# A mixer kernel on one core: unit 0's combination two scans later, the layer norm's shift one scan later, the normalising one slot later

## The reference

```python
x = x + 0.5 * ffn(layernorm(x), gate_w, experts)
x = x + mixer(layernorm(x), W_in, conv_w, conv_b, A_log, D, W_out)
x = x + 0.5 * ffn(layernorm(x), gate_w, experts)

def mixer(x, ...):
    x_ssm, res = split(x @ W_in.T)                  # 512 channels each
    x_conv = silu(causal_conv4(x_ssm) + conv_b)
    delta = softplus(x_conv)
    A_d = exp(delta[..., None] * -exp(A_log))       # 16 decays for each channel
    # for every channel and each of its 16 states, over the 2048 tokens:
    #   h = A_d[t] * h + x_conv[t]**2
    #   y[t] = x_conv[t] * sum(h over the 16 states)
    y = y * silu(res) + D * x_conv
    return y @ W_out.T
```

## Time and profile before

| | us |
|---|---|
| median of 3 runs | 3705.03 (3700.34 to 3710.84) |
| span of the profiled execution | 3705.3 |
| VectorE busy | 3111.1 (84%) |
| TensorE busy | 2776.9 (75%) |
| ScalarE busy | 2127.6 (57%) |
| GpSimd busy | 1324.0 (36%) |
| 512 scans on VectorE, line 1187 | 2224.4, 4.40 each |
| the chain that ends last | through the last layer |

### The profile page before, as it was taken

One profiled execution on the slowest core, in us unless ns is written; L12 is line 12 of the kernel. 1 busy time (PEld: TensorE's weight loads), 2 busy tenths in 40 slices (PEclk: granted clock), 3 DMA queues, 4 the chain that ended last, 5 costly groups with the idle time before them and its releaser, 6 DMA issues. The chain is left out here.

```text
span 3705.3 us, 29659 instructions
## 1 busy us (share of the span) xinstructions
PE 2776.9 (75%) x9252; PEld 1528.0 (41%) x9252; DVE 3111.1 (84%) x2547; ACT 2127.6 (57%) x2285; POOL 1324.0 (36%) x894
## 2 busy tenths in 40 slices
PE   8702688899889889889979979997896696035553
PEld 4502343354346346435534634543452455024442
DVE  6797579999999999999999999999999667982222
ACT  6300567876877777787687788778767362001111
POOL 0002265446245344534624434460111100035665
PEclk9655799999999899999989999999999896567776
DMA  7202277688678778868877787885686571034667
GB/s 276 106 0 81 78 174 178 144 182 185 150 165 161 178 163 177 191 135 173 179 162 170 158 180 160 177 193 118 127 153 132 113 282 83 0 117 132 218 221 244
DMA packets 146186, 575.75 MB, mean 155 GB/s; under 512 B 22096, under 2 KB 73872, under 8 KB 99216
## 3 DMA queue, kind: packets, MB, share of 16 engines
q0 software_dynamic: 76704, 400.61, 52.1%
q1 hardware_dynamic: 69360, 173.68, 12.7%
HBM read 154.72 MB, written 119.60 MB: 74 GB/s over the span
## 5 line engine op out<-in xcount | busy, mean ns | idle before, releaser
L1187 DVE TENSOR_TENSOR_SCAN state<-state,drive 128x2048 f32<-128x2048 f32 x512 | 2224.4, 4402 | 53.8 <-ACT state L1393 53.6
L1393 ACT ACTIVATE state<-delta,neg_a 128x2048 f32<-128x2048 f32 x512 | 1018.9, 2004 | 213.3 <-DMA delta<-xc 85.5
L1644 PE MATMUL ps_states<-state,ident 128*128 128x512 f32 x1792 | 843.2, 615 | 82.1 <-DMA state<-state 67.1
L1068 POOL DMA_DIRECT2D state<-state x255 | 235.6, 924 | 1299.9 <-DVE state L1187 1289.5
L1546 PE MATMUL ps_proj<-x1t,w_in 128*128 128x512 f32 x1024 | 507.3, 640 | 86.3 <-ACT xc L1342 30.4
L1644 PEld LDWEIGHTS ps_states<-state,ident 128*128 128x128 f32 x1792 | 344.5, 198 | 478.3 <-issue 381.6
L1562 PE MATMUL ps_proj<-conv_in,tap 128*128 128x512 f32 x1024 | 490.9, 631 | 53.6 <-ACT conv_in L1306 32.6
L997 POOL DMA_INDIRECT picked<-normed_rows,slot_now x112 | 356.7, 3185 | 95.0 <-PE ps_rows L1527 49.4
L1013 POOL DMA_INDIRECT x<-routed_rows,row_now x112 | 346.4, 3093 | 34.6 <-issue 34.6
L1546 PEld LDWEIGHTS ps_proj<-x1t,w_in 128*128 128x128 f32 x1024 | 204.2, 204 | 366.8 <-issue 273.2
L1562 PEld LDWEIGHTS ps_proj<-conv_in,tap 128*128 128x128 f32 x1024 | 205.0, 203 | 320.5 <-issue 281.9
(11 more groups left out here) (299 smaller groups left out, 3240.1 us busy)
## 6 DMA issues: line engine op xcount, KB each, us to landing
state<-state POOLq DMA_DIRECT2D x255, 1024.0 KB, 7.0
delta<-xc POOLq DMA_DIRECT2D x24, 1024.0 KB
normed_rows<-rows_in SPq DMA_DIRECT2D x8, 2048.0 KB
x_rows<-x SPq DMA_DIRECT2D x16, 1024.0 KB, 7.7
normed_rows<-rows_mid SPq DMA_DIRECT2D x8, 2048.0 KB
f_total<-x_rows SPq DMA_DIRECT2D x8, 2048.0 KB
routed_rows<-f_routed SPq DMA_DIRECT2D x128, 128.0 KB
out<-f_total SPq DMA_DIRECT2D x8, 2048.0 KB
```

Source lines behind the costliest of these rows:

```text
L1068: nc.gpsimd.dma_start(out=state[held(q)][:], in_=state[held(q - 1)][:], accum_op=ALU.add).then_inc(pair_landed(b, q // 2)[0], 16)
L1187: nc.vector.tensor_tensor_scan(state[held(q)][:], state[held(q)][:], drive[j % 2][:], 0.0, ALU.mult, ALU.add).then_inc(state_ready, 1)
L1393: nc.scalar.activation(state[held(q)][:], delta[j % 2][:], ACT.Exp, scale=g.neg_a[:, j, n:n + 1]).then_inc(decay_ready, 1)
L1644: mm = nc.tensor.matmul(ps_sum[c][:], g.ident[:], state[held(q)][:, c * CH:(c + 1) * CH], start=(opening and n == 1), stop=(n == N - 1))
```

## The change

Three numbers. Unit 0's combination stands behind scan 24 instead of 22. Both calls of `scales` (the shift) stand one scan later. Both normalisings start one slot later, with the slot of `deviation` as it was.

```diff
-    GATE, COMBINE = (3, 3, 4, 4), (6, 4, 6, 4)
+    GATE, COMBINE = (3, 3, 4, 4), (8, 4, 6, 4)
...
                         if q == SCALE[i]:
                             aggregate(b + 1, i)
-                        if q == SCALE[i] + 2:
+                        if q == SCALE[i] + 3:
                             scales(b + 1, i)
...
                             if q == SCALE[i] + 3:
                                 deviation(b + 1, i)
                             for t in range(TH):
-                                if q == SCALE[i] + 4 + t // 4:
+                                if q == SCALE[i] + 5 + t // 4:
                                     normalise(b + 1, i * TH + t)
```

## The result

| | before | after |
|---|---|---|
| median of 10 runs, us | 3703.99 (3689.77 to 3710.84) | 3715.7 (3703.76 to 3727.61) |
| span of the profiled execution | 3705.3 | 3713.7 |

The ratio of the changed kernel to the one before is 1.0037, with a 95% interval of 1.0023 to 1.0052: slower by 11.7 us on the medians and by some 14 us by the ratio, whose interval is about 9 to 19 us. The prediction was 3717.0 in a range of 3703 to 3729. Of the 19 runs of the kernel before that stand beside e5 to e8 one took 5033.5 us at a granted clock of 0.553, and the ratios leave it out.

The account below looks back on a forecast made before the run. The path was taken to go through GpSimd and DMA, not VectorE's own work. Batch terms (+4.2; +9.2 for 1, 5, 6; +3.2; -1.9 and -1.4; -1.3) gave +12.0 on 3705.3: 3717, range 3703 to 3729.

Parts of the forecast that it names:

- The path: Each batch runs through GpSimd's gathers, x, the DMA queue, `delta` and ScalarE's decays; `delta` lands 27.67 us behind x.
- Rival 3: The DMA queue absorbs x's delay and `delta` lands as now: about +0.3 us a batch, 3707 us; chance 0.07.
- The lock: A GpSimd gather that meets a running VectorE scan gets going only when the scan ends, ending about 0.84 us later.
- w: VectorE's wait for TensorE's last output projection before unit 0's combination; 0.88 to 2.97 us in batches 1 to 6.
- S: The moment scan 22 of a batch ends on VectorE, from which the times within that batch are counted.
- the free case: Gather of row 9 starts ahead of scan 26, takes 0.98 us, x issued at 17.4; border at w = 2.27.
- Rival 4: Scans don't hold up gathers, descriptor queue room does; x issued at 13.9, some 30 us faster, 3675 us; chance 0.10.
- Which gathers are free: Count of row 9 gathers ahead of scan 26: two, batches 2 and 4 (-1.9, -1.4 us); one or two: chance 0.36.
- locked: Gather of row 9 held until scan 26 ends; x 3.25 us later for w above 1.05, 3.4 for w = 0.88.
- rival 1: All gathers of row 9 locked, w below 2.27 throughout: +21.4 us in sum, 3727 us; chance 0.14.
- Batch 0: First batch, no wait before the combination: x issued at 20.4 instead of 16.06, 4.4 later, less 0.2: +4.2 us.
- Shift and normalising: VectorE's shift one scan and ScalarE's normalising one slot later: -0.2 us a batch, bounds -1.1 and +1.5.

Follow-up runs that it names:

- e5: Kernel before with GpSimd's transfer of x issued ahead of the gather of piece 8, nothing else moved: 3687.55 us, ratio 0.997.
- e8: Kernel before with only unit 0's combination moved, three scans later, behind scan 25: 3734.81 us against 3700.27, ratio 1.0087.
- e4: Changed kernel with GpSimd's transfer of x issued ahead of the gather of piece 8: 3679.72 us, ratio 0.9942 to the kernel before.
- e1: Kernel before with only unit 0's combination moved, behind scan 24: 3714.96 us against 3702.69, ratio 1.0036.
- e7: Changed kernel with 1.71 us of unused VectorE statistics added behind scan 25: 3698.86 us against the kernel before's 3700.27, ratio 1.0002.
- e9: Kernel before with the combination behind scan 24 and x issued ahead of the gather of piece 8: 3669.74 us, ratio 0.9907.
- e3: Kernel before with only unit 0's combination moved, one scan later, behind scan 23: 3683.94 us, ratio 0.9949.
- e2: Kernel before with only the shift one scan and the normalising one slot later: 3702.38 us, ratio 1.0001.
- e6: Kernel before with the combination behind scan 23 and x issued ahead of the gather of piece 8: 3659.6 us, ratio 0.989.
- e10: Kernel before with the combination behind scan 23, x ahead of the gather of piece 8, shift and normalising later: 3660.79 us, ratio 0.9889.

## Where the prediction held, and where not

**The path** (gathers of pieces 8 and 9, x, queue, `delta`, decays). Held. 13.9 of the 15.5 us by which the batches grew are landings; x to `delta` is 27.6 us as before in batches 1 to 6. Rival 3, that the queue absorbs the shift, would have had the landing at 46.1 in batch 5; it was at 47.9. e4 adds its limit: moving x alone earlier leaves the state transfer behind it where it was, and only part is handed on.

**The lock.** Held in its numbers. Gather 8 ends 5.20 us behind the combination's end (5.2 forecast), x follows 9.5 us behind it in batches 1 to 6. The prediction wrote that last as 10.8 for w = 2.31, or 20.4 behind S for small w, and w was small: 20.35. Gather 8 begins 1.0 us behind the combination's end and not 0.7; scan 25 hides the difference. In e1 the free case came out at 17.4 to the tenth, with the border case, w = 2.26, on the free side. Rival 4 needs gathers of about 1 us inside a running scan, with the descriptor queue's room as what held them. The interval from the state transfer's issue to the gather's end is 2140.29 - 2129.28 = 11.0 and 15.3 us after, where it was 4.58 and 8.84; no fixed room does this, and both gathers end 0.8 to 0.9 us behind scans as before. e7 closes it.

**Which gathers are free: this step failed.** The forecast carried each batch's w over from the trace of before and counted two free. After, w is 0.85 to 1.06 in all of batches 1 to 6, and all six are locked: rival 1's pattern. Rival 1 gave +22.7 for batches 0 to 6 though, and they grew by 15.5. Batch 0, which was not locked, makes 3.4 of the difference. The other cause is w: locked, x stands at 20.4 whatever w is below 1.05, so the price is 20.4 less where x stood before (w + 16.1), and not w + 19.4 less that. Over batches 1 to 6 the x transfers came 12.6 us later in sum and not 19.7; the growth that the landings don't explain, below, hides part of that. I had taken w out of the difference, as if it would be the same on both sides.

Part of where w comes from can be read in the row of TensorE's first eight convolutions after a pause of 4.4 us for ScalarE, some 110 us ahead of the combination that waits. Before, ahead of batch 6's w of 2.16 (2.27 by VectorE's wait):

```profile
2321.82 6.71 PE L1562 MATMUL ps_proj<-conv_in,tap 128*128 128x512 f32 x8 [4.44 <-ACT conv_in L1306]
```

and after, ahead of batch 6's w of 0.85:

```profile
2330.72 5.39 PE L1562 MATMUL ps_proj<-conv_in,tap 128*128 128x512 f32 x8 [4.45 <-ACT conv_in L1306]
```

The same eight matmuls, 1.32 us apart, and w is 1.31 apart. Stretches of 4 us over them, first of before and then of after: length; busy of PE, PEld, DVE, ACT, POOL; PEclk, DMA share, GB/s:

```profile
2322.00:2326.00 4.00, 4.00 (x5) 1.68 (x6) 4.00 (x3) 2.31 (x3) 1.81 (x2) 0.50 1.02 256
2326.00:2330.00 4.00, 4.00 (x8) 1.62 (x7) 4.00 (x2) 1.43 (x2) 2.50 (x1) 0.76 1.02 209
```

```profile
2331.00:2335.00 4.00, 4.00 (x6) 1.60 (x6) 4.00 (x3) 2.20 (x2) 1.92 (x2) 0.61 1.06 262
2335.00:2339.00 4.00, 4.00 (x14) 2.25 (x13) 4.00 (x2) 2.86 (x4) 2.39 (x1) 1.00 1.08 217
```

The granted clock is 0.50, the 1.2 GHz level, when TensorE takes up work after the pause. In the kernel before it stayed there for all of the first stretch; in the changed one it was back at 1.00, 2.4 GHz, sooner (0.61 is a mean over both levels). Over batches 1 to 6 of the twelve profiles a block of 5.1 to 5.4 us goes with w between 0.8 and 1.4, and one of 5.95 to 6.8 us with w of 1.65 to 3.0, but for four: 5.17 us with 2.95 (e1, batch 5), 5.19 with 2.93 (e8, batch 2), 5.48 with 2.48 (e7, batch 1) and 5.40 with 2.95 (e9, batch 5). So the time that the clock takes to come back after this pause goes with w in most batches, and it is not the only source of it. That the change made w small is not shown: e1, with the same combination, has three large ones.

**Batch 0.** Forecast +4.2, measured +0.8. This step failed too. The term came from "locked", since w is zero there. VectorE and GpSimd in batch 0 after:

```profile
578.88 8.74 DVE L1187 TENSOR_TENSOR_SCAN state<-state,drive 128x2048 f32<-128x2048 f32 x2 [2.41 <-ACT state L1393]
```

```profile
573.00 4.33 POOL L1013 DMA_INDIRECT x<-routed_rows,row_now  x1 [5.62 <-DVE xc L1168]
577.63 0.98 POOL L1013 DMA_INDIRECT x<-routed_rows,row_now  x1 [0.30 <-issue]
578.57 1.06 POOL L1022 DMA_DIRECT2D x<-in_x  x1
```

Scan 26 waits 2.41 us for its decay and starts at 17.6, so the gather, there at 16.4, is free. In the trace of before that decay ended at 15.1, which would have locked it. 1.5 of the 2.5 us between them lies again with TensorE behind a pause: eight matmuls that sum states, ahead of the projection that ScalarE waits for. Before and after:

```profile
565.10 3.67 PE L1644 MATMUL ps_states<-state,ident 128*128 128x512 f32 x8 [3.15 <-ACT ps_states L1335]
```

```profile
562.96 5.20 PE L1644 MATMUL ps_states<-state,ident 128*128 128x512 f32 x8 [3.15 <-ACT ps_states L1335]
```

The windows over their first 3.5 us, before and after:

```profile
565.10:568.61 3.51, 3.51 (x9) 1.60 (x10) 3.51 (x2) 3.40 (x4) 3.21 (x2) 1.00 0.73 149
```

```profile
562.96:566.50 3.54, 3.54 (x5) 1.67 (x6) 3.54 (x2) 3.41 (x4) 3.54 (x2) 0.56 0.54 111
```

The granted clock is 1.00 in the one and 0.56 in the other, behind the same pause of 3.15 us. e1, e3 and e8 have 5.18 us there, e2, e4, e5, e6, e7, e9 and e10 3.67. So both places where the forecast had the wrong side of the lock, this one and w, go in part with how soon the clock came back. No run here varies the clock alone.

**Shift and normalising.** Forecast -0.2 a batch, between -1.1 and +1.5; e2 says nothing within 0.15%. In batch 5 the shift's wait of 2.08 us goes, and 0.66 us comes back at once as a wait before scan 32 (0.9 forecast). The rest was paid back at unit 1's gate, with 2.15 us, a place that the prediction did not name. From the landing to the next S, batches 1 to 6 took 265.8 to 266.1 us after, and 264.5 to 267.9 before; e1, without these edits, has 266.0 to 267.2 where locked and 264.9 to 265.3 where free. So nothing points to these edits as the source of the 1.6 us that the landings don't explain. What it is due to stays open.

**The sum.** +12.0 was forecast and 11.7 measured, and the nearness flatters it. Against the batches' 15.5: batch 0 was 3.4 too high; batches 1 and 2 were given +3.05 and -1.9 and came to +0.5 and +1.0; batch 3 had +3.2 and got it; batch 4 was given -1.4 and came to +3.1; 5 and 6 were given 6.1 and came to 6.8. The forecast for batches 0 to 6 was 13.3, and it came that near by errors of both signs. Batch 7 was to give back 1.3; its wait before the combination is gone, but the stretch from there on varies by more. Right were the mechanism, the sign and, once the side of the lock is known, each position of x to 0.1 us; the count of free gathers was a guess on a quantity that isn't steady. Also open: e1 had three free gathers in its profiled execution and the changed kernel none, which makes 10 us up to batch 7's S, and yet their spans (3713.0 and 3713.7) and medians (3714.96 and 3715.7) are the same; the part behind S of batch 7 was 970 us in the one and 961 in the other.

## What to carry over

When a VectorE instruction moves, look at what GpSimd's queue does behind the semaphore that it raises: a wait removed on VectorE came back as a late transfer, and the better step was one scan and not two, since with one the buffer came free within 0.2 us of being asked for, inside a scan that held the gather anyway. In an in-order queue put the large transfer on which the others depend ahead of those that may wait, here for 13 to 36 us by moving one issue. A wait read from one execution is worth carrying into a forecast only if it repeats where nothing has changed; w did not: it lay between 0.8 and 3.0 us from batch to batch.

## What the runs showed of the hardware that was not expected

- A gather by index is held for the rest of a running scan. Over the twelve profiles 1129 of those into `x1` begin inside a scan, and all but one end 0.78 to 0.89 us behind a scan's end, after 3.96 us for instance in place of 0.98; the one begins in the same instant as its scan and takes 1.05 (in e1 another such takes 5.27). The combination holds them in the same way (2.92 us). Direct transfers issued on the same queue inside scans take 0.90 us in the median, and those over 1.1 us (up to 1.7) are the ones that begin before the transfer ahead has ended. So not every DMA issue of GpSimd's is held; those by index are.
- Inside the gate, which reads PSUM and one SBUF tensor, the same gather takes 0.98 us, and begun beside `bn_stats` 1.00 us. More work on VectorE, 1.71 us a batch, made the changed kernel 13 to 17 us faster (e7).
- The same eight matmuls after the same pause of 4.4 us take 5.39 us in one execution and 6.71 in another, or 5.20 and 6.65 in one (e1, pauses of 4.64 and 4.72), with the granted clock of the first pair at 0.61 and 0.50 over a first stretch and 1.00 and 0.76 over the next. Eight others after 3.15 us take 3.67 or 5.20 us, at a clock of 1.00 or 0.56.
- From the issue of x to the landing of `delta` it takes 27.6 us where the state transfer of scan 25 is issued 0.6 us behind x. With x alone 12.5 us earlier it takes 34.6 (e4), and with that transfer at 16.0 us too, 32.0 (e6). The queue hands a delay on in full, and the advance of one of its transfers only in part.
